# The seventh group's weighting and sums are moved behind the last dense piece, and the second half's first slot between closing slots

## The reference, cut to what matters

```python
x = x + layernorm(gated_scan(layernorm(x)))     # a recurrent layer
x = x + layernorm(experts(layernorm(x)))        # 32 experts, 4 chosen for each token
# experts(x), for token t:
logits = x @ gate_w.T; scores = sigmoid(logits)
ids = top_k(scores + e_bias, 4); w = scores[ids] / sum(scores[ids])
combine[t, ids] = w
g, u = einsum('th,ehi->tei', x, w1), einsum('th,ehi->tei', x, w3)
out = einsum('tei,eih->th', silu(g) * u * combine, w2)
```

## Time and profile before

| | |
|---|---|
| median of 3 runs | 341.75 us |
| the profiled execution | 343.86 us |
| its span, first to last instruction | 342.1 us |
| PE / DVE / POOL / ACT busy | 283.5 / 257.1 / 236.2 / 217.8 us |
| instructions | 6589 |

### The profile page before, as it was taken

One profiled execution on the slowest core, in us unless ns is written; L12 is line 12 of the kernel. 1 busy time (PEld: TensorE's weight loads), 2 busy tenths in 40 slices (PEclk: granted clock), 3 DMA queues, 4 the chain that ended last, 5 costly groups with the idle time before them and its releaser, 6 DMA issues.

```text
span 342.1 us, 6589 instructions
## 1 busy us (share of the span) xinstructions
PE 283.5 (83%) x1515; PEld 224.0 (65%) x1516; DVE 257.1 (75%) x976; ACT 217.8 (64%) x546; POOL 236.2 (69%) x272
## 2 busy tenths in 40 slices
PE   4575687587674999999998989999999999999760
PEld 2244254454453889889886988888776766898540
DVE  3878679878989477787448978744578887867796
ACT  6938766988683555556554555555588678765672
POOL 4395777777777777777743777777777777777700
PEclk9965666866965699999999999999999999999995
DMA  3999999961111556667646999876511121521222
GB/s 98 313 306 287 280 279 281 307 172 51 47 54 55 155 161 197 185 198 223 200 140 172 250 253 268 236 206 179 148 52 53 47 54 49 141 59 52 67 77 61
DMA packets 83999, 54.81 MB, mean 160 GB/s; under 512 B 8032, under 2 KB 80512, under 8 KB 83968
## 3 DMA queue, kind: packets, MB, share of 16 engines
q1 hardware_dynamic: 57472, 30.85, 33.1%
q0 software_dynamic: 6912, 14.17, 14.5%
q10 hardware_dynamic: 19584, 9.44, 9.8%
HBM read 25.07 MB, written 29.36 MB: 159 GB/s over the span
## 4 chain that ended last, share of the span: by engine, by line
PE 38%; POOL 17%; DVE 13%; ACT 11%; issue 11%; DMA 5%; SPq 4%; POOLq 0%; ACTq 0%; DVEq 0%
POOL xs_dram L404 17%; PE bank L1676 6%; PE bank L1667 6%; PE bank L1672 6%; PE bank L1594 4%; PE bank L1626 3%; SPq L305 3%; DMA xb<-xs_dram 3%; PE bank L1462 3%; PE bank L1495 2%; PE bank L1607 2%; PE bank L1589 2%; PE bank L1455 2%; ACT L460 2%; DVE at_at L1351 1%
## 5 line engine op out<-in xcount | busy, mean ns | idle before, releaser
L413 POOL DMA_INDIRECT yk<-ys_dram,row_ys x108 | 107.4, 994 | 41.5 <-issue 26.8
L404 POOL DMA_INDIRECT xs_dram<-xn_all,row_xs x108 | 108.6, 1006 | 36.2 <-issue 32.3
L1594 PE MATMUL bank<-w,xbT 128*128 x288 | 60.5, 333 | 0.3 <-ACT xbT L617 0.2
L617 ACT COPY xbT<-bank 128x256 f32<-128x256 f32 x72 | 26.8, 373 | 33.1 <-PE bank L1589 29.7
L1092 DVE TENSOR_TENSOR act_a<-silu,bank 128x192 f32<-128x192 f32 x72 | 25.4, 353 | 29.9 <-ACT silu L620 26.2
L1594 PEld LDWEIGHTS bank<-w,xbT 128*128 128x128 f32 x288 | 46.0, 194 | 1.1 <-issue 0.9
L1626 PE MATMUL bank<-w2s,aT 96*128 x288 | 46.0, 282 | 0.1
L1626 PEld LDWEIGHTS bank<-w2s,aT 96*128 96x128 f32 x288 | 37.7, 191 | 2.4 <-issue 1.4
L1676 PE MATMUL bank<-at_at,xn_all 128*128 128x384 f32 (+1 forms) x96 | 34.8, 444 | 4.0 <-DVE at_at L1351 3.9
L1101 DVE COPY yb<-bank 128x256 f32<-128x256 f32 x72 | 30.4, 422 | 8.5 <-PE bank L1626 6.8
L620 ACT ACTIVATE silu<-bank 128x192 f32<-128x192 f32 x72 | 23.8, 331 | 20.1 <-PE bank L1594 19.4
(11 more groups left out here) (216 smaller groups left out, 532.8 us busy)
## 6 DMA issues: line engine op xcount, KB each, us to landing
xb<-xs_dram SPq DMA_DIRECT2D x144, 64.0 KB
ys_dram<-yb ACTq DMA_DIRECT2D x72, 128.0 KB, 2.6
xs_dram<-zeros SPq DMA_DIRECT2D x2, 2048.0 KB, 15.0
ys_dram<-zeros SPq DMA_DIRECT2D x1, 2816.0 KB, 13.4
ys_dram<-zeros SPq DMA_DIRECT2D x1, 2560.0 KB, 18.2
x_sb<-in_L_attn_x_dram SPq DMA_DIRECT2D x8, 256.0 KB, 5.8
xs_dram<-xn_all,row_xs POOLq DMA_INDIRECT x108
yk<-ys_dram,row_ys POOLq DMA_INDIRECT x108, 2.5
```

Of the source, the lines that this page charges most:

```text
L404: pool.indirect_dma_start(out=xs[h], out_offset=bass.IndirectOffsetOnAxis(ap=row_xs[:, j, k:k + 1], axis=0), in_=xn2_all[:, j, :], in_offs ...
L413: pool.indirect_dma_start(out=yk[h][:, j - h * TP, k, :], out_offset=None, in_=ys[h], in_offset=bass.IndirectOffsetOnAxis(ap=row_ys[:, j, ...
L617: act.copy(xbT[:, p, :, :].rearrange("c b t -> c (b t)"), ps_xbT[p][:, 0:2 * P]).then_inc(b_xc[h], 1)
L1594: ins = pe.matmul(ps_gu[o][:, b * 2 * I:(b + 1) * 2 * I].rearrange("t (w a i) -> t w a i", w=2, a=1), xbT[:, o, b, :], w13[:, :, bass.ds(e ...
```

## The change

Group 6: ACT weights three tiles instead of two and DVE one instead of two; all of it, and the first sum, comes out of the pieces and behind piece 47. The order of the statistics at the end becomes: dense tiles, group 6, group 7. At the turn between the halves, `slot(1, 0)` goes ahead of closing slot 2 of the first half on PE and ACT, and on ACT `slot(1, 1)` goes ahead of closing slot 3. DVE's order at the turn stays.

```diff
-                (TP + 2 * GT, TP + 3 * GT, G), (TILES + LEFT[1].start, TILES + D, G + 1), ...
+                (TILES + LEFT[1].start, TILES + D, G), (TP + 2 * GT, TP + 3 * GT, G + 1), ...
@@ by_act
-            return GT // 2 if g == G - 2 else routed(g) - 1 if g == G - 1 else routed(g)
+            return routed(g) - 1 if g >= G - 2 else routed(g)
@@ scalar
+            def behind(h, t):
+                slot(h, most[h] * BODY + 3 * BODY + t, t, stages(left=t))
...
                     slot(h, t, t % BODY, stages(t))
+                    if h and t < 2:
+                        behind(0, t + 2)
...
-                for t in range(4):
-                    slot(h, most[h] * BODY + 3 * BODY + t, t, stages(left=t))
+                for t in range(2 if h == 0 else 4):
+                    behind(h, t)
@@ scalar, between(e)
-                if e in (44, 45):
-                    weighted(6, e - 44)
@@ scalar, behind the pieces
+            for j in range(by_act(6)):
+                weighted(6, j)
+                if j == 1:
+                    turned_back(1)
             act.preload_act_table(ACT.Sqrt)
-            turned_back(1)
             for j in range(by_act(7)):
                 weighted(7, j)
             root_last(3)
             root_last(4)
             for n in range(2):
-                norm_last(6, 3, n)
+                norm_last(6, 4, n)
@@ vector, between(e)
-                if 42 <= e < 46:
-                    weigh_in_6(e - 42)
-                if e == 47:
-                    two_sums(6, by_act(6))
@@ vector, behind the pieces (after; done and waits on c_sum left out)
+            m, n = by_act(6), by_act(7)
+            for k in range(K):
+                weigh_in(6, m, k)
             for k in range(K):
-                if k == K - 1:
-                    stats_d(1)
-                    spread_d(1)
                 weigh_in(7, n, k)
+            stats_d(1)
+            spread_d(1)
+            two_sums(6, m)
+            one_sum(6, m)
+            bn(lambda j: gathered(6)[:, j, 0, :], st3)
+            aggregate(st3, mv3[:, 6 * GT:7 * GT, :])
+            inverse_last(3)
             two_sums(7, n)
             dve.bn_stats(st3[:, n, :], gathered(7)[:, n, 0, :])
             one_sum(7, n)
+            inverse_last(4)
             bn(lambda j: gathered(7)[:, j, 0, :], st3, n)
             aggregate(st3, mv3[:, 7 * GT:7 * GT + n + 1, :], n + 1)
-            inverse_last(3)
-            inverse_last(4)
             norm_d(1)
@@ tensor
                     slot(h, t, t // BODY, t % BODY, stages(t))
+                    if h and t == 0:
+                        behind(0, 2)
...
-                for t in range(BODY):
-                    slot(h, most[h] * BODY + 3 * BODY + t, most[h] + 3, t, stages(left=t))
+                for t in range(2 if h == 0 else 3):
+                    behind(h, t)
```

More of the change, by code:

```diff
@@ L161, in sandwich_kernel @@
         st_d = [sb(f"st_d{n}", [P, w // P, 6]) for n, w in enumerate(WIDE)]
-        LAST = [(0, TH[0], GH), (TP, TP + 2 * GT, GH + 3), (TILES, TILES + LEFT[0].stop, GH + 2), (TP + 2 * GT, TP + 3 * GT, G),
-                (TILES + LEFT[1].start, TILES + D, G + 1), (TP + 3 * GT, TP + TH[1], G + 2)]
+        LAST = [(0, TH[0], GH), (TP, TP + 2 * GT, GH + 3), (TILES, TILES + LEFT[0].stop, GH + 2), (TILES + LEFT[1].start, TILES + D, G),
+                (TP + 2 * GT, TP + 3 * GT, G + 1), (TP + 3 * GT, TP + TH[1], G + 2)]
         LATE = [3, 4, 5, 6]
@@ L1317, in weigh_in @@
                     dve.scalar_tensor_tensor(out=first_row, in0=row, scalar=w, in1=first_row, op0=ALU.mult, op1=ALU.add).then_inc(c_sum, 1)
[L1319 to L1326, removed]
             def two_sums(g, n):
@@ L1352, in _ @@
                 between(e)
[L1353 to L1363, removed]
+            m, n = by_act(6), by_act(7)
+            dve.wait_ge(s_yk[6], 16 * GT * K)
+            dve.wait_ge(v_wt, G)
+            for k in range(K):
+                ge(dve, c_sum, k and done + k)
+                weigh_in(6, m, k)
+            done += K
             dve.wait_ge(s_three, 16 * (K - 1))
@@ L1372, in _ @@
             done += K
+            stats_d(1)
+            spread_d(1)
+            two_sums(6, m)
+            dve.wait_ge(c_sum, done + 1)
+            one_sum(6, m)
+            dve.wait_ge(c_sum, done + 2)
+            dve.wait_ge(c_ve, G)
+            bn(lambda j: gathered(6)[:, j, 0, :], st3).then_inc(c_sum, 1)
+            dve.wait_ge(c_sum, done + 3)
+            aggregate(st3, mv3[:, 6 * GT:7 * GT, :]).then_inc(c_ve, 1)
+            inverse_last(3)
+            done += 3
             two_sums(7, n)
-            dve.wait_ge(c_ve, G)
-            dve.wait_ge(c_sum, done)
+            dve.wait_ge(c_ve, G + 1)
             dve.bn_stats(st3[:, n, :], gathered(7)[:, n, 0, :]).then_inc(c_sum, 1)
@@ L1629, in slot, with behind @@
                     ins.then_inc(b_y[h], 1)
+            def behind(h, t):
+                slot(h, most[h] * BODY + 3 * BODY + t, most[h] + 3, t, stages(left=t))
             for h in range(HALVES):
```

## The result

The forecast was 342.2 us (340.9 to 343.3), no change or a little slower. Over 19 runs each, the changed kernel took 345.08 us (median) and the kernel before 342.84: ratio 1.0060, 95% interval 1.0040 to 1.0079, slower by about 2.0 us. The first three runs of the kernel before, on which the forecast stood, had the median 341.75; about 1.1 us of the distance between 342.2 and 345.08 is that. Against the ratio, the forecast was 1.0013, and 1.6 us are missing.

What follows compares the result with a forecast made beforehand. Prediction: a block's landing bounds the turn, DVE the pieces up to about 323 us and everything behind piece 47. End +1.45 - 0.99 = +0.46, turn 0; added to the 341.75 us median this gave 342.2 us (340.9 to 343.3).

Steps and rivals of the forecast that it cites:

- Pieces 43 to 47: Last pieces: with group 6's weightings gone from DVE, piece 47's second multiplication comes 0.99 us earlier (bounds 0 and 1.87).
- Behind piece 47: End: one tile's weighting and two longer sums on DVE, less a stall, cost net 1.45 us; ACT stays hidden.
- The turn: Between the halves: reordering on PE and ACT nets 0 us (bounds -0.9 and +0.45).
- come later by what the transposes take: Turn: closing slot 2's product, its copy and DVE's work behind it come at least 0.22, about 0.45 us later.
- the 0.92 us for which PE waits at 197.58: Behind the turn: PE's wait for a block was to cover the 0.45 us lost, net 0.
- rival D: Turn: added idleness lowers TensorE's clock, 3 us of work at half speed cost about 3 more; 344.7 us, chance 0.04.
- A: Last pieces: they don't speed up because DVE's residuals hold the last two; end 1.45 us later, 343.2 us, chance 0.08.
- B: Behind the turn: the load landing at 197.58 comes earlier; about 341.7 us, or 341.3, chance 0.15.
- C: Gathers behind the turn's late store come later than taken; a 4 us delay costs 1.7, giving 343.9 us; chance 0.05.
- the prediction's own signs of being wrong: Pieces starting over 0.5 us off, gather waits reaching PE, PEclk below 1.00 between 180 and 330, or ACT late at the end.

Runs made afterwards that it cites:

- tail_only: The kernel before with only the change's hunks at the end, the turn as before: 343.27 us, ratio 1.0021 to the kernel before.
- turn_first: Only the change at the turn, with DVE's six weight steps moved ahead of closing slot 2's copy: 343.29 us, ratio 1.0020 to the kernel before.
- tail_less: Only the change at the end, without DVE's weighting of group 6's last tile (summed unweighted): 342.99 us, ratio 1.0011 to the kernel before.
- in_pieces: The kernel before with ACT weighting three tiles of group 6 and DVE one, inside the pieces, nothing moved behind piece 47: 343.02 us, ratio 1.0019.
- turn_only: The kernel before with only the change's hunks at the turn, the end as before: 344.85 us, ratio 1.0063 to the kernel before.
- turn_warm2: Only the change at the turn, plus 10 identity transposes on PE ahead of slot (1, 0) and 16 in slot (1, 2): 344.81 us, ratio 1.0046.
- before_spread: The kernel before with DVE's six weight steps spread: two ahead of slot (1, 1), two behind it, two behind slot (1, 2): 343.05 us, ratio 1.0000.
- turn_pe: The kernel before with only PE's new order at the turn, ACT's order and the end as before: 344.79 us, ratio 1.0074.
- turn_act: The kernel before with only ACT's new order at the turn, PE's order and the end as before: 342.77 us, ratio 1.0009.
- before_late: The kernel before with 1.3 us more on DVE (two unused multiplications) behind the six weight steps at the turn: 344.79 us, ratio 1.0067.
- pause_new_warm: pause_new with 20 more identity transposes on PE in slot (1, 2): 345.02 us, ratio 1.0064 to the kernel before.
- act_spread: The kernel before with ACT's new order at the turn and DVE's six weight steps spread as in before_spread: 343.16 us, ratio 1.0013.
- full_spread: The whole change with DVE's six weight steps spread: two left, two behind slot (1, 1), two behind slot (1, 2): 344.38 us, ratio 1.0038.
- pause_new: Only the change at the turn, plus 40 identity transposes on PE in closing slot 0 of the first half: 348.41 us, ratio 1.0168.
- pause_old: The kernel before plus 40 identity transposes on PE in closing slot 0 of the first half: 346.24 us, ratio 1.0127.

## Why the prediction was wrong
**Pieces 43 to 47, right.** Forecast -0.99; the stretch from the first dense product to piece 47's second multiplication is 85.22 us instead of 86.21, and 85.23 in tail_only.

**Behind piece 47, right, a little small.** Forecast +1.45, measured +1.65 (1.64 to 1.66 in the four profiles that have it). A tile's weighting takes 1.35 and not 1.20; the sums of 768 and 384 elements took 0.92 and 0.56, forecast 0.95 and 0.55. Net +0.66 in place of +0.46, and tail_only's 0.7 us agree. In the pieces the mechanism was right too, and not only the sum: piece 46's second multiplication and the silu of 47 come where the prediction put them.

**The turn, wrong.** The step that failed is "come later by what the transposes take, at least 0.22 ... and, since the second block must have landed, about 0.45", and with it "the whole is covered by the 0.92 us for which PE waits at 197.58". Measured between the last two copies it is 1.82 us in the profile after (2.59 instead of 0.77), and 1.5 to 5.0 in the five others of this order without a pause (turn_first, whose DVE order differs, left out). Three things were in its place:

1. The term was mis-sized. In the profile after, 0.71 us of waiting for both blocks, 0.66 of transposes and the 0.52 without a visible cause, which I had not counted at all, make it up. And I took the lateness of the blocks from one execution. There PE came to slot (1, 0) when its blocks had landed: 0.57 us lie between the copy before the last and the first transpose. In the old order this distance runs up to 1.2 (tail_only), 2.2 (tail_less) and 3.75 us (in_pieces), in the new one from 0.12 (after) to 2.0 (turn_only) and 3.2 (turn_warm2). What varies most is PE's own arrival: that copy lies 1.8 (in_pieces) to 6.2 us (before_spread) behind the last scatter, while a first block that PE waits for is transposed 4.4 to 5.6 us behind it. Why PE arrives so differently is not shown. In the old order DVE has its last copy and does its 3.6 us of other work in this wait; in the new one that begins after it. turn_pe and turn_act show that it is PE's order, and turn_first that most of the loss goes when this DVE work stands ahead of the copy.
2. The cover of 0.92 us was used up and was too small. In the profile after, PE's transposes behind DVE's product start 11.25 us behind the last scatter instead of 10.16, 1.1 us later, and the clock takes about 1.4 more: 2.5 against 0.92. The trace after has no wait for a block between 190 and 216 us. That leaves 1.6 of the 2.1 us between the two profiles; 0.5 are not accounted for.
3. The idleness that is left lies in one piece, and the clock falls in the busy slots behind it. This was my rival D, at 0.04 and 3.0 us; its mechanism came, at about half its price. I had priced the added idleness at 0.45 us, on top of two waits; it was 2.36 in one. But a fall is no mark of the new order: of nine profiles with PE's old order and no pause five have one between 180 and 188 us (tail_only, in_pieces, tail_less, turn_act, before_late, 3.4 to 6.9 us long), and tail_less, in_pieces and turn_act can't be told from the kernel before in time.

How the 2 us divide between the delay and the clock stays open: turn_first removes both together, the kernels that should keep the clock alone came too late for it, and pause_new_warm doesn't isolate it. Two of the prediction's own signs of being wrong came true, the start of the pieces and a PEclk below 1.00 behind 180 us.

**Rivals.** A (no gain in the pieces) is refuted by 85.22. B (blocks land earlier, a gain) didn't show; PE came too late in the profile after to wait for that block. C's first half holds, gathers move with the store. Its price is in four profiles, turn_act, turn_first, act_spread and full_spread: ACT waits 1.65 to 1.71 us for group 4's rows and the pieces take 0.6 to 0.7 us longer. In the profile after there was no such wait: the pieces began 60.5 us behind the first gather, in turn_act 57.3.

## What to carry to other kernels
Before an instruction is put behind one that waits for data, list what stands behind it on the next engines: here one product moved by a place took 3.6 us of unrelated DVE work out of a wait that had hidden it. A margin at a meeting of two independent chains must not be read from one execution; here it ran from 0.57 to 3.75 us in one order of the instructions. And where a stretch differs by up to 3 us between single profiles of kernels whose medians are less than 1 us apart, the runs have to say what a change did to it, and not two profiles.

## What was not expected of the hardware
TensorE's granted clock fell to 0.50 behind one idle stretch of 2.63 us (pause_new) and not behind two of just under 1 us with about 1.9 us of work between them (pause_old). Nor is it the single wait that decides: it fell in before_late behind waits of 0.91, 0.42 and 0.46 us, when PE had been busy 1.26 of 3.00 us. With 2.2 us of the idleness filled with transposes it stayed at 1.00 (pause_new_warm).
